# Attention scores by four 64x64 TensorE tiles without the masked quadrants, values four units behind

## The chip, the cores and the metric

The kernel runs on one core of one Trainium2 chip. The metric is the device time of one execution in microseconds (us). Engines are named as in the profile: PE is TensorE's matmul side and PEld its weight loads, DVE is VectorE, ACT ScalarE, POOL GpSimd, SP SyncE.

## What is computed

Three layers on x of shape (4, 2048, 256): a feed-forward layer with ternary weights, attention, and the same feed-forward layer again. The change touches the attention alone:

```python
q = einsum('bld,dhk->blhk', x, Wq) / sqrt(dh)      # 16 heads of 64
k = einsum('bld,dhk->blhk', x, Wk)
v = einsum('bld,dhk->blhk', x, Wv)
# side keys and values: x summed over groups of 16 tokens, 128 groups a batch
# block of 128 queries against 3 * 128 neighbouring keys and 128 side keys
rel = k_idx - bl - q_idx
valid = (abs(rel) <= 127) & (k_pos >= 0) & (k_pos < L)
logits = einsum('bnqhd,bnkhd->bnhqk', qb, k_cat) + bias   # 0, or -1e9 where not valid
probs = softmax_with_extra_logit(logits)
y = einsum('bnhqk,bnkhd->bnqhd', probs, v_cat)
out = einsum('blhk,hkd->bld', y, Wo)
```

A query at place i of its block sees the keys of the left block from place i + 1 on and those of the right block up to place i - 1. So of the left block's keys the first 64 are masked for the last 64 queries, and of the right block's keys the last 64 are masked for the first 64 queries. These are the masked quadrants.

## The kernel before

**Tiling.** The attention works through 64 blocks of 128 tokens, 16 to a batch, in rounds of four blocks (`RING`), so 16 rounds. One head of one block is a unit: 16 units a block, 1024 in all. All loops are written out, so every unit has instructions of its own. Numbers are split in two f16 parts, high and low, and each product is three passes (high x high, high x low, low x high).

**One head.** PE makes the scores of four key tiles of 128 (left, own, right, side, in an order that depends on the block's place in the round, `order_of`) into one of four PSUM banks `score_ps`, 512 columns. DVE adds the mask and takes the largest (L1354). ACT makes the exponentials (L1286). The high part is a copy, by ACT (L1302) for three heads of four and by DVE (L1366) for the fourth. POOL makes the low part (L1013). SP issues one DMA that turns the eight 128x128 f16 tiles of the head (L987); all such issues are on SP's one queue, one behind the other. PE multiplies the turned tiles with the values (`values`, L1147), 12 matmuls of 64 columns. The first block of a batch has no left tile and the last no right one, so three key tiles each.

**How far ahead.** In unit u, SP is to turn head u + 1, POOL to split head u + 2, ACT to make the exponentials of u + 3, DVE to take the largest of u + 4. PE makes the scores of u + 4 to u + 7 in every fourth unit (two pairs of heads), and the values of u - 3 (`PV_LAG`). There are six buffers for the turned tiles, so the issue of head v waits until the values of v - 6 are done.

**The items.** Between these steps PE makes the block's projections in pieces, one or two a unit (`PIECES`): V1, Q0, Q1, K0, K1, V0 for the coming block, OUTP for the one before, and three transposes: XTR turns the normalised x of the block after the next, YT1 and YT0 turn the two halves of y. XTR and YT1 use the bank `y_ps[1]`, which also holds the values of heads 8 to 15. K0 needs XTR's result, the output projection's third piece needs YT1's. Four side items (SK0, SK1, SV0, SV1) come only where a batch begins or ends. `FIRST_ORDER` and `LAST_ORDER` give the items' numbers there. Each item's result is copied out by ACT (high part, L1263) and DVE (low part, L1346).

**Scores in detail.** `scores` takes two heads at once: the even head lies on partitions 0 to 63 of queries and keys, the odd one on 64 to 127, so the two matmuls of a step use the two row halves of the array, 64 rows by 128 columns each. Key tiles that lie side by side in the ring are taken in one matmul. The keys are stored as `k_parts[P, slot, part, HD]`. Every matmul has its own weight load.

**y.** DVE inverts the denominators in units 2 and 10 of a block and scales y in units 3 and 11 (`normalise_y`, L1408).

Of the kernel before, what the change touches and what calls it, by code (L numbers as in the profile page):

```python
# [6 lines left out]
F16 = mybir.dt.float16  # L7
# [8 lines left out]
P = 128  # L16
# [4 lines left out]
H, DH = 16, 64  # L21
# [676 lines left out]
def attention_phase(nc, w):  # L698
# [20 lines left out]

    V1, Q0, XTR, Q1, YT1, K0, OUTP, K1, YT0, V0 = PLAIN = range(10)
    SK0, SK1, SV0, SV1 = range(10, 14)
    FIRST_ORDER = [SK1, V1, Q0, XTR, Q1, SV1, YT1, K0, OUTP, K1, YT0, V0]
    LAST_ORDER = [V1, Q0, XTR, Q1, YT1, K0, SK0, OUTP, K1, YT0, V0, SV0]
    BANK_OF = {V1: 0, Q0: 1, Q1: 0, K0: 0, OUTP: 1, K1: 0, V0: 1, SK1: 1, SV1: 1, SK0: 0, SV0: 0}

    SIDE_LAST, RIGHT_FIRST, OWN_FIRST = ORDERS = ((LEFT, OWN, RIGHT, SIDE_TILE), (RIGHT, LEFT, OWN, SIDE_TILE),
                                                  (OWN, RIGHT, LEFT, SIDE_TILE))
    MASK_OF = {SIDE_LAST: 0, RIGHT_FIRST: 4, OWN_FIRST: 3}  # L730
    PIECES = [[(V1, 0)], [(V1, 1)], [(Q0, 0)], [(Q0, 1)], [(XTR, 0), (Q1, 0)], [(Q1, 1)], [(OUTP, 0)], [(OUTP, 1), (YT1, 0)],
              [(K0, 0)], [(K0, 1)], [(OUTP, 2)], [(OUTP, 3)], [(K1, 0)], [(K1, 1)],
              [(YT0, 0), (V0, 0)], [(V0, 1)]]
    XTR_SLOT = 4
    FIRST_SIDE = {0: SK1, 5: SV1}
    LAST_SIDE = {10: SK0, 15: SV0}
    TURNS = (XTR, YT1, YT0)
# [6 lines left out]
    U = RING * H  # L744
    ROUNDS = BLK_PER_BATCH // RING
    STATS_SLOT, NORM_SLOT = 6, 14
    SCORE_AHEAD, EXP_AHEAD, SPLIT_AHEAD, TURN_AHEAD, PV_LAG = 4, 3, 2, 1, 3
    NBUF = 4
    NPARTS = 6
    CLEARED = 4  # L750
# [8 lines left out]
    with ExitStack() as ctx:  # L759
# [14 lines left out]
        xn = sb("b_x_normed", [P, D], F32)  # L774
        xt = [sb(f"b_xT{n}", [P, KD, 2, P], F16) for n in range(2)]
        qs = sb("q_parts", [P, 2, 2, HD], F16)
        kr = sb("k_parts", [P, RING + 1, 2, HD], F16)
        vr = sb("v_parts", [P, RING + 1, 2, HD], F16)
        probs = [sb(f"probs{n}", [P, 4 * P], F32) for n in range(NBUF)]
        parts_of = [sb(f"probs_split{n}", [P, 2, 4 * P], F16) for n in range(NPARTS)]  # L780
# [39 lines left out]

        var_done, rstd_done, xn_done = sem("b_var_done"), sem("b_rstd_done"), sem("b_xn_done")
        dve_step, cleared, half_set = sem("b_dve_step"), sem("b_cleared"), sem("half_set")
        y_cleared = sem("y_cleared")
        block = ctx.enter_context(nc.Block())

        class At:
# [124 lines left out]
        def tiles_of(at, v):  # L951

            j, place = v // H, place_of(at, v)
            slots = {LEFT: (j - 1) % RING, SIDE_TILE: SIDE, OWN: j % RING, RIGHT: (j + 1) % RING}
            tiles = [(t, slots[key]) for t, key in enumerate(order_of(at, v))]
            return tiles if place == INNER else tiles[1:]

        def flat(at, v):

# [88 lines left out]
        def _(pe):  # L1048
# [53 lines left out]
            def scores(at, v):  # L1102

                j, h = divmod(v, H)
                pair, place = h // 2, place_of(at, v)
                if v >= NBUF:
                    max_done.wait(pe, at.heads + v + 1 - NBUF)
                if h == 0 and v:
                    pe.wait_ge(lo_done, at.item(j - 1, SK0 if place == FIRST else K0) + 1)
                if h == H // 2:  # L1110
                    pe.wait_ge(lo_done, at.item(j, SK1) + 1 if place == FIRST else at.item(j - 1, K1) + 1)
                cols = slice(pair * P, (pair + 1) * P)
                todo, started = tiles_of(at, v), False
                while todo:

                    (t, slot), n = todo[0], 1
                    while n < len(todo) and todo[n][1] == slot + n:
                        n += 1
                    todo = todo[n:]
                    for q_part, k_part in ((HI, HI), (HI, LO), (LO, HI)):  # L1120
                        ends = not todo and q_part == LO
                        even = nc.tensor.matmul(score_ps[v % NBUF][:, t * P:(t + n) * P],  # L1122
                                                qs[0:DH, j % 2, q_part, cols], kr[0:DH, slot:slot + n, k_part, cols],
                                                start=not started, stop=ends, skip_group_check=True)
                        odd = nc.tensor.matmul(score_ps[v % NBUF + 1][:, t * P:(t + n) * P],  # L1125
                                               qs[DH:P, j % 2, q_part, cols], kr[DH:P, slot:slot + n, k_part, cols],
                                               start=not started, stop=ends, skip_group_check=True)
                        started = True
                even.then_inc(scores_done.sem, 1)
                odd.then_inc(scores_done.sem, 1)  # L1130

# [52 lines left out]
            for index, (kind, n) in enumerate(PRE):  # L1184
                if index == FIRST_SCORES:
                    pe.wait_ge(lo_done, FIRST_SCORES)
                    for v in range(0, SCORE_AHEAD, 2):
                        scores(At(0, 0), v)
                if kind == XTR:
                    turn_x(y_ps[0], n)  # L1190
                    continue
                earlier = [m for m in range(index) if PRE_ORDER[m] not in TURNS]
                if len(earlier) > 1:
                    bank_free(index, index - earlier[-2])
                pe.wait_ge(lo_done, PRE.index((XTR, n)) + 1)
                project(kind, pre_bank(index), side_source(0) if kind in (SK0, SV0) else block_source(n))

            def body(at, b):
                for u in range(U):
                    j, h = divmod(u, H)  # L1200
                    if u % NBUF == 0:
                        for pair in range(0, NBUF, 2):
                            scores(at, u + SCORE_AHEAD + pair)
                    side = side_item(at, j, h)
                    if side == SK1:
                        block_item(at, b, j, side, (0, 1))
                    for kind, piece in PIECES[h]:
                        if kind not in TURNS:
                            block_item(at, b, j, kind, (piece,))
                    if h == XTR_SLOT:  # L1210
                        block_item(at, b, j, XTR, (0,))
                    if side in (SK0, SV0, SV1):
                        block_item(at, b, j, side, (0, 1))
                    values(at, u - PV_LAG)
                    for kind, piece in PIECES[h]:
                        if kind in (YT0, YT1):
                            block_item(at, b, j, kind, (piece,))
# [3 lines left out]
            pe.wait_ge(lo_done, PRE_ITEMS)  # L1221
            batches(pe, body)
            end = End()
            values(end, -3)
            values(end, -2)
            values(end, -1)
# [4 lines left out]
        def destination(kind, part, xt_parity, slot):  # L1231

            c = int(kind in SECOND)
            if kind == XTR:
                return xt[xt_parity][:, :, part, :]
            if kind in KEYS:
                return kr[:, slot, part, 512 * c:512 * c + 512]
            if kind in QUERIES:
                return qs[:, slot, part, 512 * c:512 * c + 512]
            if kind in VALUES:  # L1240
                return vr[:, slot, part, 512 * c:512 * c + 512]
            return yt[:, part, 4 * c:4 * c + 4, :]

        def result(kind, bank):
            if kind == XTR:
                return bank[:, 0:KD * P].rearrange("p (k n) -> p k n", k=KD)
            return bank[:].rearrange("p (c n) -> p c n", c=4) if kind in (YT0, YT1) else bank[:]

        def ring_slot(j, kind):

# [79 lines left out]
        def _(dve):  # L1330
# [83 lines left out]
            nc.vector.memset(yt[:, :, 0:NPAIR // 2], 0.0).then_inc(cleared, 1)  # L1414
            statistics(0)
            normalise_x(0, None)
            dve.sem_inc(y_done.sem, 1)
            for index, (kind, n) in enumerate(PRE):
                if index == FIRST_SCORES:
# [17 lines left out]
            def body(at, b):  # L1437
                count["base"], count["n"] = at.round * PER_ROUND + before, 0
                for u in range(U):
                    j, h = divmod(u, H)  # L1440
                    if u % NBUF:
                        split_high(at, u + SPLIT_AHEAD)
                        largest(at, u + SCORE_AHEAD)
                    for n, kind in due(at, u):
                        item(at, n, kind)
                    if u % NBUF == 0:
                        split_high(at, u + SPLIT_AHEAD)
                        largest(at, u + SCORE_AHEAD)
                    if h == STATS_SLOT:
                        moments(at.blocks + j + 3)  # L1450
                    if h == STATS_SLOT + 1:
                        mean_variance()
                        add_eps()
                    if h == NORM_SLOT:
                        normalise_x(at.blocks + j + 3, at.item(j, XTR) + 1)
                    if h in (2, 10):
                        invert_denominators(at, u - 3)
                    if h in (3, 11):
                        normalise_y(at, u - 4, at.before(j) if h == 3 else at.item(j, YT1) + 1)
                    for n, kind in due_late(at, u):  # L1460
                        item(at, n, kind)
                assert count["n"] == PER_ROUND
# [37 lines left out]
```

## Time and profile before

| | us |
|---|---|
| median of 3 runs | 2176.99 |
| lowest, highest | 2176.89, 2182.71 |
| the profiled execution | 2183.18 |
| its span, as the profile has it | 2181.5 |

In the span, the first feed-forward layer runs to about 308 us, the attention from there to about 1922 us, the second feed-forward layer after it. The granted TensorE clock is 0.991 of full speed in the mean. Busy shares over the span: PE 94%, PEld 72%, DVE 86%, ACT 88%, POOL 64%.

How to read it: a busy share says how long an engine had something in it, not that it set the pace. Several engines here are near 90%. A wait in the profile belongs to the engine that stood still, and names what ended it. SP's queue isn't counted as busy at all, and its issues have to be looked at one by one: an issue row gives its start and its length, and a second view the time from issue to landing.

### The profile page before, as it was taken

How to read it: one execution, taken by the hardware profiler on the slowest of the kernel's cores; microseconds unless marked ns; L12 is line 12 of the kernel's file. 1: busy time of each engine (PE TensorE's matmuls, PEld its weight loads, DVE VectorE, ACT ScalarE, POOL GpSimd, SP SyncE). 2: the span in 40 equal slices, each digit the busy share in tenths (PEclk: the TensorE clock that was granted, in tenths of full speed). 3: DMA queues.
4: the chain of work that ended last, by engine and by line, in shares of the span. 5: the costliest groups of instructions: out<-in, count | busy, mean ns of one | idle time of the engine just before them, and what ended most of it. 6: DMA issues, size and time to landing. Idle time of an engine off the chain costs nothing. (4 is left out here: it accounts for less than half of the span.)

```text
span 2181.5 us, 77479 instructions
## 1 busy us (share of the span) xinstructions
PE 2049.6 (94%) x30286; PEld 1567.5 (72%) x30286; DVE 1879.6 (86%) x4646; ACT 1930.1 (88%) x4210; POOL 1406.1 (64%) x1455
## 2 busy tenths in 40 slices
PE   5999979999999999999999999999999999979999
PEld 3666657777777777777777778777777777746666
DVE  7999968889998898898979899998889889867776
ACT  5899958999999899999989999998999999969997
POOL 2444536777787687777767777786777777722221
PEclk9999989999999999999999999999999999989999
DMA  7888837999999899999989999999999999958998
GB/s 210 154 156 153 158 61 124 172 166 176 171 173 171 132 174 170 172 178 168 171 143 162 172 174 169 178 179 152 149 171 172 169 177 175 163 87 177 179 179 182
DMA packets 1341581, 355.54 MB, mean 163 GB/s; under 512 B 1321760, under 2 KB 1340192, under 8 KB 1341216
## 3 DMA queue, kind: packets, MB, share of 16 engines
q1 hardware_dynamic: 1341216, 350.59, 100.4%
q8 instruction: 239, 3.92, 0.7%
q14 instruction: 126, 1.03, 0.2%
HBM read 14.68 MB, written 8.39 MB: 11 GB/s over the span
## 5 line engine op out<-in xcount | busy, mean ns | idle before, releaser
L1013 POOL TENSOR_TENSOR probs_split<-probs,probs_split 128x512 f16<-128x512 f32 (+1 forms) x1026 | 1159.3, 1130 | 385.3 <-ACT probs_split L1302 281.3
L1286 ACT ACTIVATE probs<-probs,minus_max 128x512 f32<-128x512 f32 (+1 forms) x1027 | 717.0, 698 | 27.1 <-DVE minus_max L1354 26.9
L1354 DVE CUSTOM_DVE_ANT_0 probs<-score_ps,mask,neg_qk_scale 128x512 f32<-128x512 f32 (+1 forms) x1028 | 723.5, 716 | 9.6 <-PE score_ps L1125 8.3
L1147 PEld LDWEIGHTS y_ps<-v_parts,probsT 128*128 128x128 f16 x11904 | 457.7, 98 | 149.4 <-DMA probsT<-probs_split 71.1
L1147 PE MATMUL y_ps<-v_parts,probsT 128*128 128x64 f16 x11904 | 514.8, 193 | 51.4 <-DMA probsT<-probs_split 49.8
L1302 ACT ACTIVATE probs_split<-probs 128x512 f16<-128x512 f32 (+1 forms) x770 | 470.2, 611 | 8.5 <-DMA probsT<-probs_split 0.3
L1122 PE MATMUL score_ps<-k_parts,q_parts 64*128 64x384 f16 (+3 forms) x2604 | 371.1, 286 | 4.7 <-DVE k_parts L1346 2.7
L1125 PE MATMUL score_ps<-k_parts,q_parts 64*128 64x384 f16 (+3 forms) x2604 | 371.1, 286 | 0.0
L1122 PEld LDWEIGHTS score_ps<-k_parts,q_parts 64*128 64x128 f16 x2604 | 200.5, 94 | 108.0 <-issue 13.2
L1054 PE MATMUL item_ps<-b_xT,wk_split 128*128 128x128 f16 x3168 | 221.7, 220 | 1.9 <-DVE v_parts L1346 1.5
L1054 PE MATMUL item_ps<-wo_split,yT_parts 128*128 128x256 f16 x1560 | 213.9, 274 | 6.1 <-DVE v_parts L1346 4.6
L1054 PE MATMUL item_ps<-b_xT,wq_split 128*128 128x128 f16 x3120 | 218.2, 220 | 1.2 <-DVE b_xT L1346 0.9
L1054 PE MATMUL item_ps<-wv_split,b_xT 128*128 128x512 f16 x786 | 212.3, 380 | 0.0
L1054 PEld LDWEIGHTS item_ps<-b_xT,wk_split 128*128 128x128 f16 x3168 | 180.3, 98 | 35.7 <-issue 22.1
L1366 DVE CAST probs_split<-probs 128x512 f16<-128x512 f32 (+1 forms) x256 | 181.0, 707 | 27.8 <-ACT probs L1286 27.7
L1125 PEld LDWEIGHTS score_ps<-k_parts,q_parts 64*128 64x128 f16 x2604 | 200.4, 94 | 0.0
L1286 ACT ACTIVATION_READ_ACCUMULATOR probs<-probs,minus_max 128x1 f32 x1027 | 194.2, 189 | 0.0
L1054 PEld LDWEIGHTS item_ps<-b_xT,wq_split 128*128 128x128 f16 x3120 | 178.6, 98 | 18.7 <-issue 12.9
L1054 PEld LDWEIGHTS item_ps<-wo_split,yT_parts 128*128 128x128 f16 x1560 | 135.7, 98 | 19.5 <-DVE v_parts L1346 5.1
L1346 DVE TENSOR_TENSOR yT_parts<-y_ps,yT_parts 128x512 f16<-128x512 f32 x129 | 88.5, 686 | 54.4 <-ACT yT_parts L1263 54.3
L1346 DVE TENSOR_TENSOR v_parts<-item_ps,v_parts 128x512 f16<-128x512 f32 x140 | 95.7, 686 | 43.5 <-ACT v_parts L1263 43.4
L1263 ACT ACTIVATE k_parts<-item_ps 128x512 f16<-128x512 f32 x141 | 84.2, 597 | 53.8 <-PE item_ps L1054 51.5
(172 smaller groups left out, 3452.1 us busy)
## 6 DMA issues: line engine op xcount, KB each, us to landing
probsT<-probs_split SPq DMA_TRANSPOSE x1025, 3.9
out_x<-x_resident SPq DMA_DIRECT2D x64, 128.0 KB, 2.0
x_resident<-in_L_attn_x SPq DMA_DIRECT2D x56, 128.0 KB, 2.7
h_a<-in_L_ffn_w_up SPq DMA_DIRECT2D x1, 1024.0 KB, 5.8
scratch_a<-in_L_ffn_w_down SPq DMA_DIRECT2D x1, 1024.0 KB, 8.0
x_resident<-in_L_attn_x SPq DMA_DIRECT2D x2, 512.0 KB, 9.4
raw_q_a<-in_L_attn_Wq SPq DMA_DIRECT2D x1, 1024.0 KB, 11.5
raw_k_a<-in_L_attn_Wk SPq DMA_DIRECT2D x1, 1024.0 KB, 11.8
```

The source lines that it names most:

```text
L1013: nc.gpsimd.tensor_tensor(parts_of[ring(at, v)][:, LO, low_columns(place_of(at, v))], probs[v % NBUF][:, cols], parts_of[ring(at, v)][:, H ...
L1054: last = nc.tensor.matmul(out, left(k, a), right(k, b), start=(k == 0 and m == 0), stop=(k == n - 1 and m == 2))
L1122: even = nc.tensor.matmul(score_ps[v % NBUF][:, t * P:(t + n) * P], qs[0:DH, j % 2, q_part, cols], kr[0:DH, slot:slot + n, k_part, cols], ...
L1125: odd = nc.tensor.matmul(score_ps[v % NBUF + 1][:, t * P:(t + n) * P], qs[DH:P, j % 2, q_part, cols], kr[DH:P, slot:slot + n, k_part, cols ...
L1147: last = nc.tensor.matmul(out, pt[ring(at, v)][:, low * a + t, :], vr[:, slot, b, h * DH:(h + 1) * DH], start=(n == 0), stop=(n == len(pas ...
L1263: nc.scalar.activation(dst, src, ACT.Copy).then_inc(hi_done, 1)
L1286: nc.scalar.activation(probs[v % NBUF][:, cols], probs[v % NBUF][:, cols], ACT.Exp, bias=bias[:, j % 2, h:h + 1], scale=-1.0, accum_out=su ...
L1302: nc.scalar.activation(parts_of[ring(at, v)][:, HI, cols], probs[v % NBUF][:, cols], ACT.Copy).then_inc(phi_done[v % 4], 1)
L1346: nc.vector.tensor_tensor(dst, src, hi, ALU.subtract).then_inc(lo_done, 1)
L1354: nc.vector.tensor_tensor_reduce(out=probs[v % NBUF][:, cols], in0=score_ps[v % NBUF][:, cols], in1=mask_of(at, v), scale=w.neg_qk_scale[: ...
L1366: nc.vector.tensor_copy(parts_of[ring(at, v)][:, HI, cols], probs[v % NBUF][:, cols]).then_inc(phi_done[v % 4], 1)
```

## The change

Four edits, all in the attention:

1. `scores` cuts each matmul in two halves of the queries, so four tiles of 64 rows by 64 columns are addressed: even and odd head, first and last 64 queries. For the last 64 queries the first 64 keys of the left tile are left out, for the first 64 queries the last 64 keys of the right tile. `key_runs` finds the columns that lie side by side. The keys' layout becomes `[P, part, pair, slot * P]`, so that half a tile and its neighbour are one run; ACT and DVE write them in four pieces of 128.
2. The quadrants left out are never written by PE. So DVE clears the four `score_ps` banks once, before the first item, and PE waits for that before the first scores.
3. `PV_LAG` goes from 3 to 4: PE makes the values of u - 4 in unit u. The inversion and scaling of y move from units 2, 3, 10, 11 to 3, 4, 11, 12.
4. XTR moves from unit 4 to unit 6, ahead of OUTP's first piece, behind Q1 in the items' order; YT1 moves from unit 7 to unit 8.

```diff
-    V1, Q0, XTR, Q1, YT1, K0, OUTP, K1, YT0, V0 = PLAIN = range(10)
+    V1, Q0, Q1, XTR, YT1, K0, OUTP, K1, YT0, V0 = PLAIN = range(10)
-    FIRST_ORDER = [SK1, V1, Q0, XTR, Q1, SV1, YT1, K0, OUTP, K1, YT0, V0]
-    LAST_ORDER = [V1, Q0, XTR, Q1, YT1, K0, SK0, OUTP, K1, YT0, V0, SV0]
+    FIRST_ORDER = [SK1, V1, Q0, Q1, SV1, XTR, YT1, K0, OUTP, K1, YT0, V0]
+    LAST_ORDER = [V1, Q0, Q1, XTR, YT1, K0, SK0, OUTP, K1, YT0, V0, SV0]
-    PIECES = [[(V1, 0)], [(V1, 1)], [(Q0, 0)], [(Q0, 1)], [(XTR, 0), (Q1, 0)], [(Q1, 1)], [(OUTP, 0)], [(OUTP, 1), (YT1, 0)],
-              [(K0, 0)], [(K0, 1)], [(OUTP, 2)], [(OUTP, 3)], [(K1, 0)], [(K1, 1)],
+    PIECES = [[(V1, 0)], [(V1, 1)], [(Q0, 0)], [(Q0, 1)], [(Q1, 0)], [(Q1, 1)], [(XTR, 0), (OUTP, 0)], [(OUTP, 1)],
+              [(K0, 0), (YT1, 0)], [(K0, 1)], [(OUTP, 2)], [(OUTP, 3)], [(K1, 0)], [(K1, 1)],
-    XTR_SLOT = 4
+    XTR_SLOT = 6
-    SCORE_AHEAD, EXP_AHEAD, SPLIT_AHEAD, TURN_AHEAD, PV_LAG = 4, 3, 2, 1, 3
+    SCORE_AHEAD, EXP_AHEAD, SPLIT_AHEAD, TURN_AHEAD, PV_LAG = 4, 3, 2, 1, 4
-        kr = sb("k_parts", [P, RING + 1, 2, HD], F16)
+        kr = sb("k_parts", [P, 2, NPAIR, (RING + 1) * P], F16)
+        def key_runs(at, v, side):
+
+            order, runs = order_of(at, v), []
+            for t, slot in tiles_of(at, v):
+                first = DH if order[t] == LEFT and side == 1 else 0
+                end = DH if order[t] == RIGHT and side == 0 else P
+                to, source, n = t * P + first, slot * P + first, end - first
+                if runs and runs[-1][0] + runs[-1][2] == to and runs[-1][1] + runs[-1][2] == source:
+                    runs[-1][2] += n
+                else:
+                    runs.append([to, source, n])
+            return runs
@@ scores
-                cols = slice(pair * P, (pair + 1) * P)
-                todo, started = tiles_of(at, v), False
-                while todo:
...
-                    for q_part, k_part in ((HI, HI), (HI, LO), (LO, HI)):
-                        ends = not todo and q_part == LO
-                        even = nc.tensor.matmul(score_ps[v % NBUF][:, t * P:(t + n) * P],
-                                                qs[0:DH, j % 2, q_part, cols], kr[0:DH, slot:slot + n, k_part, cols],
-                                                start=not started, stop=ends, skip_group_check=True)
-                        odd = nc.tensor.matmul(score_ps[v % NBUF + 1][:, t * P:(t + n) * P],
-                                               qs[DH:P, j % 2, q_part, cols], kr[DH:P, slot:slot + n, k_part, cols],
-                                               start=not started, stop=ends, skip_group_check=True)
+                runs = [key_runs(at, v, side) for side in range(2)]
+                last = {}
+                for q_part, k_part in ((HI, HI), (HI, LO), (LO, HI)):
+                    for run in range(max(map(len, runs))):
+                        for side in range(2):
+                            if run >= len(runs[side]):
+                                continue
+                            queries = slice(pair * P + side * DH, pair * P + (side + 1) * DH)
+                            to, source, n = runs[side][run]
+                            ends = q_part == LO and run == len(runs[side]) - 1
+                            for odd in range(2):
+                                rows = slice(odd * DH, (odd + 1) * DH)
+                                last[odd] = nc.tensor.matmul(
+                                    score_ps[v % NBUF + odd][side * DH:(side + 1) * DH, to:to + n],
+                                    qs[rows, j % 2, q_part, queries], kr[rows, k_part, pair, source:source + n],
+                                    start=(run == 0 and q_part == k_part), stop=ends, skip_group_check=True)
@@ PE, before the first scores, and DVE, before the first item
+                    pe.wait_ge(scores_cleared, NBUF)
+            for n in range(NBUF):
+                nc.vector.memset(score_ps[n][:], 0.0).then_inc(scores_cleared, 1)
@@ DVE, each unit
-                    if h in (2, 10):
-                        invert_denominators(at, u - 3)
                     if h in (3, 11):
-                        normalise_y(at, u - 4, at.before(j) if h == 3 else at.item(j, YT1) + 1)
+                        invert_denominators(at, u - 4)
+                    if h in (4, 12):
+                        normalise_y(at, u - 5, at.before(j) if h == 4 else at.item(j, YT1) + 1)
```

## Rows read from the trace of the kernel before

**Rows 1.** Busy us (instructions): PE, PEld, DVE, ACT, POOL; clock, DMA share, GB/s

```profile
400.00:1800.00 1400.00, 1347.96 (x23400) 1068.58 (x23398) 1242.18 (x3066) 1286.54 (x3124) 1075.80 (x1075) 1.00 1.11 168
```

**Rows 2.** Waits, 400 to 1800 us: who for whom, total us, times, longest

```profile
PEld y_ps L1147 <- DMA probsT<-probs_split: 62.4, 110, 1.6
...
PE y_ps L1147 <- DMA probsT<-probs_split: 44.4, 80, 1.4
...
PEld score_ps L1122 <- DVE minus_max L1354: 5.8, 23, 0.5
```

**Rows 3.** Timeline of SP's queue: start us, us; whole attention, then single issues

```profile
327.33 1592.27 SPq L987 DMA_TRANSPOSE probsT<-probs_split  x1025
...
955.14 1.28 SPq L987 DMA_TRANSPOSE probsT<-probs_split  x1
...
956.51 1.29 SPq L987 DMA_TRANSPOSE probsT<-probs_split  x1
...
959.44 2.19 SPq L987 DMA_TRANSPOSE probsT<-probs_split  x1
...
961.72 1.28 SPq L987 DMA_TRANSPOSE probsT<-probs_split  x1
```

**Rows 4.** Tile probsT, two windows of 100 us, then landing over the attention

```profile
L987 SPq DMA_TRANSPOSE probsT<-probs_split x66: 1232/1288/2722, 799.1 to 899.6; - x66
...
L987 SPq DMA_TRANSPOSE probsT<-probs_split x65: 1232/1290/2582, 899.6 to 998.0; - x65
...
DMA to landing us min/median/max: 2.7/3.9/6.0
```

**Rows 5.** DMA traffic in the stretches of the issues at 955.14 and 959.44

```profile
DMA packets 933, 0.23 MB, mean 193 GB/s; under 512 B 933, under 2 KB 933, under 8 KB 933
...
DMA packets 620, 0.17 MB, mean 83 GB/s; under 512 B 619, under 2 KB 619, under 8 KB 619
...
q8 instruction: 1, 0.02, 2.8%
```

**Rows 6.** Queue q8: packets, MB; 400:1800, 327:1920, 800:900 and 900:1000 us

```profile
q8 instruction: 184, 3.01, 0.9%
...
q8 instruction: 209, 3.42, 0.9%
...
q8 instruction: 14, 0.23, 0.9%
...
q8 instruction: 13, 0.21, 0.8%
```

**Rows 7.** Timeline of PE: values, transposes of y, loads and matmuls of scores

```profile
900.36 0.51 PE L1147 MATMUL y_ps<-v_parts,probsT 128*128 128x64 f16 x12
...
902.99 0.64 PE L1087 MATMUL y_ps<-ident,y 128*128 128x128 f32 x4
...
904.55 0.09 PEld L1122 LDWEIGHTS score_ps<-k_parts,q_parts 64*128 64x128 f16 x1
904.55 0.09 PEld L1125 LDWEIGHTS score_ps<-k_parts,q_parts 64*128 64x128 f16 x1
...
904.67 0.22 PE L1122 MATMUL score_ps<-k_parts,q_parts 64*128 64x128 f16 x1
...
904.73 0.32 PE L1122 MATMUL score_ps<-k_parts,q_parts 64*128 64x384 f16 x1
...
904.89 0.32 PE L1122 MATMUL score_ps<-k_parts,q_parts 64*128 64x384 f16 x1
```

**Rows 8.** Groups by line and form, 300 to 1900 us: busy us, mean ns

```profile
L1147 PE MATMUL y_ps<-v_parts,probsT 128*128 128x64 f16 x11771 | 509.1, 193 | 49.9 <-DMA probsT<-probs_split 48.3
...
L1087 PE MATMUL y_ps<-ident,y 128*128 128x128 f32 x504 | 80.0, 281 | 0.0
...
L1263 ACT ACTIVATE b_xT<-y_ps 128x256 f16<-128x256 f32 x65 | 24.2, 372 | 17.0 <-PE y_ps L1080 16.8
...
L1413 DVE MEMSET y_ps<- 128x512 f32 x1 | 0.5, 485 | 0.5 <-PEq L84 0.5
```

More of the change, by code:

```diff
@@ L822, in attention_phase @@
         dve_step, cleared, half_set = sem("b_dve_step"), sem("b_cleared"), sem("half_set")
-        y_cleared = sem("y_cleared")
+        y_cleared, scores_cleared = sem("y_cleared"), sem("scores_cleared")
         block = ctx.enter_context(nc.Block())
@@ L1111, in scores @@
                     pe.wait_ge(lo_done, at.item(j, SK1) + 1 if place == FIRST else at.item(j - 1, K1) + 1)
-                cols = slice(pair * P, (pair + 1) * P)
-                todo, started = tiles_of(at, v), False
-                while todo:
[L1116 to L1119, printed above, removed]
-                    for q_part, k_part in ((HI, HI), (HI, LO), (LO, HI)):
-                        ends = not todo and q_part == LO
-                        even = nc.tensor.matmul(score_ps[v % NBUF][:, t * P:(t + n) * P],
-                                                qs[0:DH, j % 2, q_part, cols], kr[0:DH, slot:slot + n, k_part, cols],
-                                                start=not started, stop=ends, skip_group_check=True)
-                        odd = nc.tensor.matmul(score_ps[v % NBUF + 1][:, t * P:(t + n) * P],
-                                               qs[DH:P, j % 2, q_part, cols], kr[DH:P, slot:slot + n, k_part, cols],
-                                               start=not started, stop=ends, skip_group_check=True)
-                        started = True
@@ L1129, in scores @@
+                even, odd = last[0], last[1]
                 even.then_inc(scores_done.sem, 1)
@@ L1206, in body @@
                         block_item(at, b, j, side, (0, 1))
+                    if h == XTR_SLOT:
+                        block_item(at, b, j, XTR, (0,))
                     for kind, piece in PIECES[h]:
@@ L1209, in body @@
                             block_item(at, b, j, kind, (piece,))
-                    if h == XTR_SLOT:
-                        block_item(at, b, j, XTR, (0,))
                     if side in (SK0, SV0, SV1):
@@ L1223, in _ @@
             end = End()
+            values(end, -4)
             values(end, -3)
@@ L1236, in destination @@
             if kind in KEYS:
-                return kr[:, slot, part, 512 * c:512 * c + 512]
+                return kr[:, part, 4 * c:4 * c + 4, slot * P:(slot + 1) * P]
             if kind in QUERIES:
@@ L1246, in result @@
                 return bank[:, 0:KD * P].rearrange("p (k n) -> p k n", k=KD)
-            return bank[:].rearrange("p (c n) -> p c n", c=4) if kind in (YT0, YT1) else bank[:]
+            return bank[:].rearrange("p (c n) -> p c n", c=4) if kind in (YT0, YT1, *KEYS) else bank[:]
         def ring_slot(j, kind):
```

## The prediction

> **What bounds the kernel now.** I read the page's shares first, then the attention alone, its waits, and then the DMA issues one by one. The shares point at TensorE: in the 1400 us between 400 and 1800 it is busy 1347.96 us (96.3%), ScalarE 91.9%, VectorE 88.7%, at a granted clock of 1.00, the 2.4 GHz level [rows 1]. PE has 52 us of idle time there. The waits say what ends it: nearly always the landing of a transposed probability tile (44.4 us on the matmul side, 62.4 us on the weight side, the same stalls seen twice); for VectorE's maxima PE waits 5.8 us [rows 2].
>
> A late transpose can be latency or throughput. Latency: 3.9 us from issue to landing [rows 4], and PE uses a tile four units of work after SyncE's turn for it. Throughput: the 1025 issues fill 1592.27 us, 1.553 us each [rows 3], and one head is one issue. Single issues show how full that queue is. The reader is to see that the one at 955.14 takes 1.28 us and that the next starts 0.09 us after its end (956.42 to 956.51): 1.38 us a head with nothing in the way. The one at 959.44 takes 2.19 us, 0.9 more, and its successor again starts 0.09 us behind it (961.63 to 961.72) [rows 3]. In the stretch of the long one the DMA engines move 83 GB/s instead of 193, and one packet of queue q8, an instruction packet, is on them [rows 5].
>
> Whose instructions are these? Between 400 and 1800 q8 brings 3.01 MB in 184 packets [rows 6], 16.4 kB each, while PE runs 23400 matmuls and 23398 weight loads [rows 1]: 46798/184 = 254 a packet. No other engine has such numbers: q8 fetches PE's program, some 256 instructions at a time.
>
> What does a fetch cost SyncE? From 799.1 to 899.6 us lie 65 steps between issues and 14 fetches: (100.5 - 65 x 1.38)/14 = 0.77 us. From 899.6 to 998.0 lie 64 steps and 13 fetches: 0.78 us [rows 4, 6]. These hold whatever idle time the queue had. I take 0.75; as bounds 0.9, the single issue above, and 0.5, if one fetch in three falls between issues. Over the attention: 1025 x 1.38 = 1415 us and 209 fetches [rows 6] x 0.75 = 157 us, 1572 of 1592 us. In only about 20 us had SyncE's queue nothing to issue. **The transposing queue is the bound**, and PE the close second: its idle time is what the queue leaves it.
>
> **The change part by part.** *Scores.* Before, a pair of heads is 12 matmuls (6 where the key tiles lie in one run), even and odd head on the two row halves at once: the next starts 0.16 us after 384 columns and 0.06 after 128 [rows 7], so 3 x (0.16 + 0.06) = 0.66 us a pair. After, each is cut into two halves of the queries, and each half drops 64 of 512 key columns. By the runs that the code finds, a pair becomes 24 matmuls in the first, second and fourth block of a round (before 12), 18 in the third (6), 12 in the last block of a batch (6); over the phase 5208 become 11184. If the four tiles overlap, a pair lasts as long as one half: 320 columns are 0.135 us at the same rate, 3 x (0.135 + 0.06) = 0.585 us, 0.075 less, 512 x 0.075 = 38 us less PE work. PE is not the bound: 0 in the sum.
>
> *Instructions.* 5976 more matmuls and, since loads equal matmuls [rows 1], 5976 more loads are 11952 instructions, 11952/256 = 46.7 more fetches, each 0.75 us of SyncE's queue: **+35 us**; bounds +23 and +42.
>
> The Trainium skill, "Runtime: NRT & Kernel Launch", section "Instruction fetch mechanics", says that a program is refilled in blocks of 256 instructions over a DMA queue of the engine's own, and that crossing a block is "mostly hidden". The trace agrees on the 256; for the transposes on the same DMA engines it does not show the hiding. By the page the term would be 0 instead of 35.
>
> *Can the tiles overlap?* Two row halves do: weight loads and matmuls of both start within 0.01 us [rows 7]. Column halves and loads of 64 columns stand in no row. Fast end: the values' loads of 128 columns recur every (0.51 - 0.193)/11 = 0.029 us. Slow end: fp32 loads recur every (0.64 - 0.281)/3 = 0.12 us with their transposes [rows 7, 8], so 0.06 us for half the columns. With column halves loading in turn, four loads take at most 0.12 us, less than a run of 320 columns and more than one of 128: at worst 3 x (0.135 + 0.12) = 0.77 us a pair. PE has 52/1400 x 1.553 = 0.058 us to spare a head and gets 35/1024 = 0.034 more from the slower queue, 0.18 a pair: it binds only from 0.66 + 0.18 = 0.84 us a pair. I take 0, the nearer rows being the fast ones; the other side is a rival.
>
> *Values four units behind.* A tile gets 1.55 us more to land, but the queue serves no more tiles per us. It can win back the 20 us in which the queue was empty, in the fill and where a batch changes and PE has the side items too: **-12 us** (bounds 0 and -20). New wait: the issue of head v needs the values of v - 6 done. Tile v - 6 lands 6 x 1.55 - 3.9 = 5.4 us before that issue, which leaves them time; were that gone, each us would be one of the bound, for all behind it in SyncE's queue.
>
> *x turned at unit 6, YT1 at unit 8, normalisation one unit later.* K0 at unit 8 needs the turned x: four units of cover become two, 3.1 us, against two transposes and two copies, ACT's 0.37 us [rows 8] and DVE's of the same 256 columns. YT1 has two units until the output projection's third piece instead of three. Both hidden; if not, under 1 us a block, out of PE's spare time. Keys are stored in four pieces of 128, the same elements: 0.
>
> *Clearing four score banks.* Four memsets of 0.485 us [rows 8] on VectorE in the fill, partly beside PE's first transposes: **+1 us** (0 to 2).
>
> Sum: 35 - 12 + 1 = **+24 us**; bounds 23 - 20 = +3 and 42 + 2 = +44. The profiled execution took 2183.18 us, 2181.5 of it span, 6.2 us above the median of the runs. So 2207 in a profile, and 2176.99 + 24 = 2201 us as median.
>
> **The rivals.** *Faster: PE bounds.* If SyncE's long issues were waits that shrink when tiles come evenly, the extra unit removes PE's idle time (1593/1400 x 52 = 59 us) and the scores save up to 38, of which ScalarE's 91.9% lets most through, say 30: 2177 - 59 - 30 = 2088 us. For: 96.3%. Against: 0.09 us between issues, and the packet in the long one. It decides where SyncE's gaps are well over 0.09 us. 0.12.
>
> *No change.* Fetches fall between issues (0.5 us each) and all 20 us come back: +3, 2180 us. 0.18.
>
> The page's rule on fetches would give 2177 - 12 = 2165 us, for which I leave 0.05 of the 0.12 above.
>
> *Much slower: the four tiles take turns.* Column halves one after the other make 2 x 0.585 = 1.17 us a pair, 0.51 more, 261 us of PE work against its 59 + 35 us of room: +35 + 167, about 2379 us. Against: row halves overlap. It decides from 0.84 us a pair. 0.10.
>
> The Trainium skill gives a load as its columns/1.2 in ns ("TensorE: Matmul & The Clock Gate", section "LDWEIGHTS (loading the stationary operand)"), 53 ns for 64, and says that column tiling turns the fast load off ("TensorEngine Tiling (Array Packing)", "Restrictions"); 24 in turn would be 1.27 us a pair, on this rival's side.
>
> *The change doesn't do what it says.* If repeated weights were not loaded again, the fetches would grow by 23 only, about +6 us; but the loads equal the matmuls today [rows 1]. It is within the 0.18.
>
> **How the numbers follow.** Forecast 0.60, no change 0.18, faster 0.12, much slower 0.10. The range takes the sum's bounds (2180 to 2221), goes down over no change and the page's case to 2165, and up to 2245 for loads that cost PE part of its room. About 0.3%, 6.5 us, is what a measurement tells from no change: faster 0.12, same 0.18, slower 0.70.
>
> **What would show it.** Right: some 47 more q8 packets, issues 1.58 us apart in the mean with ordinary ones still at 1.29, a lower busy share of PE with longer waits for landed tiles, scores in fours 0.135 us apart. Wrong: gaps in SyncE's queue, a mean step under 1.55 us, or score pairs over 0.84 us with PE over 98% busy.

## The result and the profile after

The changed kernel takes 2211.45 us (median of 4 runs, 2209.7 to 2217.48) against 2179.85 us of the kernel before beside it: a ratio of 1.0152, 95% interval 1.0132 to 1.0172. It is slower by 1.5%, 32 us. The forecast was 2201 us and a loss of 24. The profiled execution has a span of 2208.0 us where the one before had 2181.5.

The two instruction queues on the page of the changed kernel (packets, MB, share of 16 engines), and then the packets of q8 in its attention, 400 to 1800 us:

```profile
q8 instruction: 286, 4.69, 0.9%
q14 instruction: 126, 1.03, 0.2%
...
q8 instruction: 221, 3.62, 1.1%
```

q8 has 47 packets more than the 239 it had, as 11952 more instructions of PE make it, and q14, the other instruction queue, has as many as before. Next, the changed kernel's windows view (busy us of PE, PEld, DVE, ACT, POOL, then clock, DMA share and GB/s), the line that answers to [rows 1]:

```profile
400.00:1800.00 1400.00, 1316.59 (x28184) 1107.09 (x28182) 1208.42 (x3014) 1264.29 (x3070) 1052.98 (x1056) 1.00 1.13 165
```

PE is busy for 94.0% instead of 96.3% while it runs 28184 matmuls instead of 23400; every other computing engine is less busy too, at the same clock. No engine became the bound: the whole attention got less to do per us. The timeline of SyncE's queue in the changed kernel answers to [rows 3], and the DMA traffic in the stretches of its first three single issues to [rows 5]:

```profile
327.08 1620.72 SPq L1000 DMA_TRANSPOSE probsT<-probs_split  x1025
...
959.14 1.29 SPq L1000 DMA_TRANSPOSE probsT<-probs_split  x1
...
960.53 2.15 SPq L1000 DMA_TRANSPOSE probsT<-probs_split  x1
...
962.77 1.28 SPq L1000 DMA_TRANSPOSE probsT<-probs_split  x1
```

```profile
q8 instruction: 1, 0.02, 6.8%
...
DMA packets 673, 0.17 MB, mean 86 GB/s; under 512 B 673, under 2 KB 673, under 8 KB 673
...
DMA packets 962, 0.24 MB, mean 219 GB/s; under 512 B 962, under 2 KB 962, under 8 KB 962
```

The same picture as before: an ordinary issue 1.28 or 1.29 us, the next 0.09 us behind it, and one of 2.15 us at 86 GB/s (its instruction packet began in the stretch ahead of it). The 1025 issues took 1620.72 us instead of 1592.27, **28.5 us more**, which is the loss of the profiled execution (26.5 us) and a little more. The mean step is not stretched evenly; only more issues are long: of the 1025, the trace has 223 over 1.6 us where the kernel before had 190, and 219 of them (189 before) have an instruction packet of q8 that starts in them or less than 1.4 us ahead. Nor is the pair of stretches above a chance find. Lined up on the starts of all 221 packets of q8 between 400 and 1800 us, the transposes start about 190 packets of their own in each quarter of a microsecond beforehand, and about 10 in the quarters from 1.0 to 1.5 us afterwards; over the 184 of the kernel before it is the same. In the tile view of probsT, 400 to 1800 us, the median issue is 1288 ns, as it was, and there are 890 issues where there were 906:

```profile
L1000 SPq DMA_TRANSPOSE probsT<-probs_split x890: 1209/1288/2643, 399.0 to 1799.5; - x178
```

One view seems to speak against a full queue. For the kernel before it has SyncE waiting for GpSimd's low parts half of the time:

```profile
SPq L987 <- POOL probs_split L1013: 769.5, 819, 21.1
```

That is only the last releaser that the profile could name. Matched head by head, each low part was done before its issue began, by 1.37 us in the median before and by 2.36 us after the change. So the tiles stood ready and the queue was late.

The scores themselves came out as hoped. One burst of four heads in the changed kernel, and the last matmuls of such a burst in the kernel before, which began at 904.55 [rows 7]:

```profile
920.89 1.35 PE L1137 MATMUL score_ps<-k_parts,q_parts 64*64 64x64 f16 x48
```

```profile
905.71 0.32 PE L1122 MATMUL score_ps<-k_parts,q_parts 64*128 64x384 f16 x1
```

Before, 24 matmuls took from 904.55 to 906.03, 1.48 us; now 48 take 1.35. Less the 0.19 us that the last one needs to drain, 1.29 and 1.16 us: 0.58 us a pair of heads, where 0.585 was forecast. Four tiles of 64x64 do overlap.

Waits of the changed kernel, 400 to 1800 us (who for whom, total us, times, longest):

```profile
PEld item_ps L1067 <- DVE yT_parts L1361: 59.6, 98, 1.6
PE item_ps L1067 <- DVE yT_parts L1361: 45.8, 56, 1.5
...
PEld y_ps L1160 <- DMA probsT<-probs_split: 37.0, 66, 1.3
ACT probs_split L1317 <- DMA probsT<-probs_split: 31.8, 60, 1.4
...
DVE probs_split L1381 <- DMA probsT<-probs_split: 21.2, 22, 2.0
...
PE y_ps L1160 <- DMA probsT<-probs_split: 19.2, 41, 1.0
```

PE's waits for landed tiles became shorter, not longer (44.4 and 62.4 us before, [rows 2]). With one unit more between transpose and use, the stall is met further up: ACT and DVE now wait for a landing before they may overwrite the buffer that is being turned. PE's wait for the turned y has another source in the main: it is 26.8 to 30.0 us also in the kernels below in which the transposes no longer bound.

### The profile page after: what moved, and what is told of

The parts are those of the page before. It is cut to its first block and busy times, and to the rows that moved or that the text cites. A ratio compares the mean times of both kernels' runs of the same rounds, so it can differ in the third digit from the quotient of the medians.

```text
span 2208.0 us, 89437 instructions
## 1 busy us (share of the span) xinstructions
PE 2036.7 (92%) x36262; PEld 1631.0 (74%) x36262; DVE 1868.9 (85%) x4650; ACT 1929.3 (87%) x4210; POOL 1402.8 (64%) x1455
## 5 line engine op out<-in xcount | busy, mean ns | idle before, releaser
L1317 ACT ACTIVATE probs_split<-probs 128x512 f16<-128x512 f32 (+1 forms) x770 | 470.8, 611 | 46.7 <-DMA probsT<-probs_split 37.3
L1137 PE MATMUL score_ps<-k_parts,q_parts 64*64 64x128 f16 (+6 forms) x11184 | 353.5, 266 | 11.0 <-DVE minus_max L1369 3.1
L1137 PEld LDWEIGHTS score_ps<-k_parts,q_parts 64*64 64x64 f16 x11184 | 253.7, 106 | 61.0 <-DVE minus_max L1369 24.5
L1381 DVE CAST probs_split<-probs 128x512 f16<-128x512 f32 (+1 forms) x256 | 161.4, 630 | 54.8 <-ACT probs L1301 31.6
L1361 DVE TENSOR_TENSOR q_parts<-item_ps,q_parts 128x512 f16<-128x512 f32 x130 | 89.5, 688 | 76.0 <-ACT q_parts L1278 76.0
L355 DVE TENSOR_TENSOR h_split_c<-h_c,h_split_c 128x1024 f16<-128x1024 f32 x64 | 78.4, 1225 | 58.2 <-ACT h_split_c L660 57.0
L282 POOL TENSOR_TENSOR h_rms_c<-mean_square_c,pow_exp_c 128x4 f32<-128x4 f32 x16 | 16.5, 1030 | 165.2 <-ACT scratch_c L664 165.2
```

Of the source, the lines that this page charges most:

```text
L1137: last[odd] = nc.tensor.matmul(score_ps[v % NBUF + odd][side * DH:(side + 1) * DH, to:to + n], qs[rows, j % 2, q_part, queries], kr[rows, ...
L1317: nc.scalar.activation(parts_of[ring(at, v)][:, HI, cols], probs[v % NBUF][:, cols], ACT.Copy).then_inc(phi_done[v % 4], 1)
L1361: nc.vector.tensor_tensor(dst, src, hi, ALU.subtract).then_inc(lo_done, 1)
L1381: nc.vector.tensor_copy(parts_of[ring(at, v)][:, HI, cols], probs[v % NBUF][:, cols]).then_inc(phi_done[v % 4], 1)
```

## The experiments

All ratios are to runs of the kernel before on the same chip. **Fetch theory**: the transposes bound the attention, and each fetch of 256 PE instructions takes some 0.7 us from them. Its rivals: PE bounds; or the moved items are slow.

### The scores alone

The four-tile scores and the cleared banks, with the rest as before (the main lines of the edit against the changed kernel):

```diff
-    SCORE_AHEAD, EXP_AHEAD, SPLIT_AHEAD, TURN_AHEAD, PV_LAG = 4, 3, 2, 1, 4
+    SCORE_AHEAD, EXP_AHEAD, SPLIT_AHEAD, TURN_AHEAD, PV_LAG = 4, 3, 2, 1, 3
-    XTR_SLOT = 6
+    XTR_SLOT = 4
```

> The change's four-tile scores and the cleared banks alone; values three units behind, x and y turned where the kernel before has them. Fetch theory (SyncE's transposing queue bounds, and each fetch of PE's instructions stretches one of its issues): 46.7 more fetches, each 0.5 to 0.9 us, so +23 to +42 us against the kernel before, q8 286 packets, no idle time in SyncE's queue inside a batch. Rival 1, PE bounds: about -38 us, since PE's work falls. Rival 2, it is the later values and turns that cost the time: within 6 us of the kernel before.

Measured: ratio 1.0148 (1.012 to 1.0175), 2211.36 us, q8 286 packets. The whole loss is here, +32 us by the ratio, and it comes with less work on PE's array. PE's waits for landed tiles grew, as forecast for the whole change (scores-only kernel, 400 to 1800 us; its profiled execution, 2199.69 us, was the fastest of its four):

```profile
PEld y_ps L1160 <- DMA probsT<-probs_split: 106.4, 164, 1.8
...
PE y_ps L1160 <- DMA probsT<-probs_split: 72.3, 126, 1.6
```

### The lag and the moved items alone

```diff
-    SCORE_AHEAD, EXP_AHEAD, SPLIT_AHEAD, TURN_AHEAD, PV_LAG = 4, 3, 2, 1, 3
+    SCORE_AHEAD, EXP_AHEAD, SPLIT_AHEAD, TURN_AHEAD, PV_LAG = 4, 3, 2, 1, 4
-    XTR_SLOT = 4
+    XTR_SLOT = 6
```

> The other half of the change alone: values four units behind, x turned at unit 6, y at unit 8, y scaled a unit later; scores as before. Fetch theory: q8 stays at 239 packets and the queue stays full, so only its idle time of some 20 us can come back, of which the changed kernel shows little: -12 to +3 us. Rival 1, PE bounds: -40 to -59 us, its waits for landed tiles being its loss. Rival 2, the later turn of y costs the time: +6 to +35 us.

Measured: ratio 1.0011 (0.9997 to 1.0025). PE's waits for landed tiles are all but gone, and a wait for the turned y stands in their place (lag-only kernel, 400 to 1800 us):

```profile
PE item_ps L1054 <- DVE yT_parts L1347: 29.2, 57, 1.1
...
PE y_ps L1147 <- DMA probsT<-probs_split: 1.3, 3, 0.7
```

Taken alone this run doesn't tell whether PE bounds: a gain by the later values could be hidden by a loss from the moved items, and the same kernel with the transposes relieved (below) takes 2177.32 us, only 6 us less. The cleaner comparison is the changed kernel with the scores-only kernel. They differ by the same half of the change, the ratios are 1.0152 and 1.0148, and here the changed kernel with the transposes relieved lies 40 us lower, at 2170.83. There too nothing is won by letting tiles land later, and nothing of the queue's idle time comes back.

### More instructions without the scores

The values' projection in eight matmuls of 64 columns instead of one of 512:

```diff
-                    last = parts(bank[:], source, lambda k, s: w.wqkv[2][:, s, k, cols], pieces, KD)
+                    for k in pieces:
+                        for m, (a, o) in enumerate(((HI, HI), (HI, LO), (LO, HI))):
+                            for r in range(8):
+                                last = nc.tensor.matmul(bank[:, 64 * r:64 * r + 64], source(k, a),
+                                                        w.wqkv[2][:, o, k, 512 * c + 64 * r:512 * c + 64 * r + 64],
+                                                        start=(k == 0 and m == 0 and r == 0),
+                                                        stop=(k == KD - 1 and m == 2), skip_group_check=True)
```

> The kernel before, with each matmul of the values' projection (128 x 512) cut in eight of 64 columns: the same sums, 5502 more matmuls and as many weight loads, scores untouched. PE's work grows by 48 x 0.029 - 6 x 0.216 = 0.11 us for each of 131 items, 14 us. Fetch theory: 11004/256 = 43 more fetches, +22 to +39 us, middle 30, q8 282 packets. Rival 1, PE bounds: +14 us. Rival 2, instruction fetches are hidden and PE has room: within 6 us of the kernel before.

Measured: ratio 1.0135 (1.0114 to 1.0156), +29 us, with 285 packets on q8. Two edits that share nothing but some 11000 to 12000 added PE instructions, half of them weight loads, cost the same. Per added packet: 32.3/47 = 0.69 us in the scores-only kernel, 29.4/46 = 0.64 us here. PE's own 14 us would not do. That the added loads slow the transposes by themselves, without a fetch, doesn't fit the single issues: the ordinary one keeps its length (1288 ns in the median), and 222 are over 1.6 us, all 222 of them with an instruction packet of q8.

### The transposes relieved: every fourth head not turned

```diff
             def turn_probs(at, v):
 
+                if (at.heads + v) % 4 == 3:
+                    return
...
-                pe.wait_ge(turned[ring(at, v)], turn_count(at, v))
+                src = v - int(v % 4 == 3)
+                pe.wait_ge(turned[ring(at, src)], turn_count(at, src))
```

> The kernel before without the transpose of every fourth head; that head's values are made from its predecessor's turned tiles (so its output is not the reference's), all other work stays. Fetch theory: SyncE's queue needs 769 x 1.38 + 209 x 0.75 = 1218 us and no longer bounds; PE's idle time (59 us) goes: -40 to -59 us against the kernel before, PE over 98% busy. Rival, the transposes don't bound the pace: within 10 us of it.

> The same with the changed kernel: no transpose of every fourth head, whose values come from its predecessor's tiles. Fetch theory: with the queue relieved PE bounds, and its shorter scores count: 10 to 38 us faster than the relieved kernel before, so -60 to -95 us against the kernel before. Rival, the four tiles or the moved items are slow by themselves: slower than the relieved kernel before by 10 to 30 us.

Measured: the relieved kernel before 0.9684 (0.9661 to 0.9707), 2113.14 us. 71 us are gained with PE's, DVE's and ACT's work unchanged, more than the 59 at most that I had for PE's idle time. PE's busy time had stalls in it too: it was 1347.96/23400 = 57.6 ns a matmul before and is 1393.82/24541 = 56.8 ns here. Its windows row (columns as above) shows PE at 99.6% and DMA's share at 0.87 instead of 1.11:

```profile
400.00:1800.00 1400.00, 1393.82 (x24541) 1122.35 (x24540) 1288.82 (x3212) 1337.78 (x3271) 1127.33 (x1126) 1.00 0.87 133
```

But the relieved changed kernel reached only 0.9946 (0.9926 to 0.9966), 2170.83 us: 58 us slower than the relieved kernel before, where I expected it 10 to 38 us faster and my rival 10 to 30 us slower. So the change holds a second loss, hidden as long as the transposes bound. The halves of the change, relieved in the same way, tell which part it is:

> The scores-only kernel (four-tile scores, values three units behind, turns as before) without the transpose of every fourth head, whose values come from its predecessor's tiles. Theory A: with the queue relieved the four-tile scores are a gain (two pairs took 1.153 us in the changed kernel, 1.293 before), and the changed kernel's loss in the relieved state comes from the moved items: 10 to 36 us faster than the relieved kernel before (2113 us). Theory B, the scores cost the time even then: 2150 to 2175 us.

> The lag-only kernel (scores as before, values four units behind, x and y turned later) without the transpose of every fourth head. Theory A, the moved items cost the time once the queue is relieved: 2160 to 2195 us, with PE waiting at the output projection for the turned y. Theory B: 2105 to 2120 us, as the relieved kernel before.

Measured: scores only 0.9626 (0.96 to 0.9651), 2103.56 us; lag only 0.9968 (0.9956 to 0.9979), 2177.32 us. Beside the relieved kernel before (2113) the scores gain 10 us and the moved items lose 64. In the relieved lag-only kernel PE waits for the turned y where in the relieved kernel before it hardly did, and ACT waits for PE to turn it (400 to 1800 us):

```profile
ACT yT_parts L1268 <- PE y_ps L1090: 58.6, 59, 2.1
...
PEld item_ps L1057 <- DVE yT_parts L1351: 43.3, 83, 0.6
...
PE item_ps L1057 <- DVE yT_parts L1351: 26.8, 57, 0.5
```

PE's own wait of 26.8 us is less than half of the 64, so this line alone doesn't account for them.

Unit 8 opens with the scores of four heads. YT1 in unit 8 so comes a unit and a burst later, and two units before the output projection that needs it. The last run put YT1 back to unit 7. It also moved XTR from unit 6 to unit 5, so two items differ from the relieved changed kernel (the lines of `PIECES` cut short):

```diff
-    PIECES = [... [(Q1, 0)], [(Q1, 1)], [(XTR, 0), (OUTP, 0)], [(OUTP, 1)],
-              [(K0, 0), (YT1, 0)], [(K0, 1)], ...
+    PIECES = [... [(Q1, 0)], [(Q1, 1), (XTR, 0)], [(OUTP, 0)], [(OUTP, 1), (YT1, 0)],
+              [(K0, 0)], [(K0, 1)], ...
-    XTR_SLOT = 6
+    XTR_SLOT = 5
```

> The changed kernel with x turned at unit 5 behind Q1 and YT1 back at unit 7 (values still four units behind), and, as in the other relieved kernels, without the transpose of every fourth head, whose values come from its predecessor's tiles. In unit 8 PE makes the scores of four heads first (1.15 us), so YT1 there comes a unit and a score burst later, two units ahead of the output projection that needs it. Theory A, YT1's place is what costs the moved items their 57 to 64 us: 2095 to 2120 us, PE's waits for yT_parts near 0. Theory B, it is the values' lag of four or the later scaling of y: 2150 to 2175 us as the relieved changed kernel (2171).

Measured: 0.9781 (0.9756 to 0.9806), 2133.41 us, between the two forecasts. The waits for yT_parts are small now, and another has come (400 to 1800 us):

```profile
PEld y_ps L1096 <- DVE y L1427: 41.2, 58, 0.8
PE y_ps L1096 <- DVE y L1427: 30.8, 55, 0.6
...
PEld item_ps L1070 <- DVE yT_parts L1365: 10.0, 56, 0.3
```

37 of the 58 us came back. As the wait that shrank is the one for the turned y, YT1's place is the likely cause, but XTR moved too, and no run moves YT1 alone. 30 us still lie between this kernel and the relieved scores-only one. PE's wait of 30.8 us at XTR for the scaled y would account for them, but x turned at unit 5 with y scaled a unit later is this run's own doing, so how the rest divides in the change itself (whose XTR is at unit 6) stays open.

### Is it the issuing or what lies behind it?

One wait less in SyncE's queue, with GpSimd waiting in its place:

```diff
-                pv_done.wait(sp, at.heads + v - NPARTS)
@@ split_low
+                pv_done.wait(pool, at.heads + v - NPARTS)
```

> The kernel before, with the wait for the values of v - 6 moved from SyncE's queue to GpSimd's, ahead of the low part that SyncE waits for anyway. All work and all orders stay. Before, each issue starts 0.092 us after the end of the last, with one waiting instruction of its own between; without it I expect 0.046. Fetch theory, the queue bounds: 1024 x 0.046 = 47 us less of it, of which PE's 59 us of room allow nearly all: -30 to -47 us. Rival, the queue only looks full: within 6 us of the kernel before.

> The scores-only kernel with the same moved wait. Fetch theory: the fetches' 30 us stay, the wait's 47 go, and PE has room for all of it: -12 to -22 us against the kernel before, so slower by 15 to 35 us than the kernel before with the moved wait. Rival, PE bounds as soon as the queue is shorter: faster than that one by up to 36 us.

Measured: 0.9984 (0.9968 to 0.9999) and 1.012 (1.0092 to 1.0148). My two forecasts against the kernel before (-30 to -47 us and -12 to -22 us) fell; I had named the wrong part of the queue. The difference between the two kernels held: 33 us, where 15 to 35 were forecast for the fetches. The time of the first is also what its rival said, a queue that only looks full; single issues tell the two apart. Three issues of the first kernel, and its tile view, 400 to 1800 us:

```profile
950.83 1.34 SPq L986 DMA_TRANSPOSE probsT<-probs_split  x1
...
952.21 1.33 SPq L986 DMA_TRANSPOSE probsT<-probs_split  x1
...
953.58 1.33 SPq L986 DMA_TRANSPOSE probsT<-probs_split  x1
```

```profile
L986 SPq DMA_TRANSPOSE probsT<-probs_split x910: 1209/1336/2742, 398.4 to 1799.8; - x182
```

The gap between issues fell from 0.09 to 0.04 us, as expected, and the issue itself grew from 1288 to 1336 ns. The step stays at 1.38 us. A queue with time to spare would have shown the 48 ns as idle time; here the issue took them up. So SyncE is held by what takes its transposes, and an issue's length is partly a wait for that. The pace of 1.38 us for a head of eight tiles is then one of the DMA side, and the fetches of instructions cut into that pace, not into SyncE's time. Which part of the DMA side sets it, no run tells.

Two heads in one issue of 16 tiles, on the changed kernel and on the lag-only one:

```diff
-                for u in range(U):
-                    turn_probs(at, u + TURN_AHEAD)
+                for u in range(0, U, 2):
+                    turn_probs(at, u)
...
+                sp.dma_start_transpose(pair_turned[n][:], pair_parts[n][:].rearrange("p h s n -> p (h s n)")).then_inc(turned[n], 16)
```

> The changed kernel with the tiles of two heads turned by one DMA issue of 16 tiles (two issues of one head each in the first and last block of a batch); six buffers as before. Same result, same bytes. If an issue costs SyncE a fixed time (an issue of 6 tiles took 1.21 to 1.24 us and one of 8 tiles 1.29), 16 tiles take about 1.5 us, the queue is half empty and PE bounds: -60 to -95 us against the kernel before. Rival, the DMA engines are the bound, not the issuing: an issue takes 2.6 us and the time stays within 15 us of the changed kernel's.

> The same two-heads issue with the scores of the kernel before (values four units behind, as in the lag-only kernel). With a fixed time for an issue: -30 to -59 us against the kernel before, and slower than the two-heads kernel with four-tile scores by 10 to 38 us. Rival, the DMA engines are the bound: within 15 us of the kernel before, and faster than the two-heads kernel with four-tile scores by some 30 us.

Measured: 1.0207 (1.0184 to 1.023), 2227.95 us, and 1.0173 (1.0153 to 1.0193), 2220.95 us. No gain came, so both forecasts for a fixed time of an issue fell. Of the rival's, one held: by the ratios the first kernel is some 12 us from the changed one (within 15). The second is 38 us slower than the kernel before, not within 15, and 7 us faster than the first, not 30. The second kernel's issues of two heads (first line) and of one head, 400 to 1800 us:

```profile
L1001 SPq DMA_TRANSPOSE probsT<-probs_split x394: 1315/2017/3542, 401.7 to 1798.4; - x197
...
L997 SPq DMA_TRANSPOSE probsT<-probs_split x96: 1209/1237/2792, 710.4 to 1575.1; - x96
```

16 tiles can be issued in 1.3 us, the median is 2.0, less than 2 x 1.38 and than the rival's 2.6. The queue has gaps here, of 0.60 us in the median over the attention where they were 0.09 before, so the loss comes from elsewhere. What it is was not tested: both kernels contain the moved items with their hidden loss, and with six buffers ACT waits 46.1 us for landings in this stretch. Whether larger issues help with the old item order and more buffers stays open.

## Why the prediction was right, and where not

**What bounds.** Right in substance. That PE at 96% was only second is shown from three sides: less PE work made the kernel slower (scores only), fewer transposes made it faster by 71 us, and later use of the tiles did nothing (changed kernel against scores only). The step that failed is the naming of the place: "1.38 us a head with nothing in the way" was read as SyncE's own 1.29 us of issuing and 0.09 us between. The kernel with one wait less showed that only the sum of 1.38 is fixed. The forecast did not depend on it, since it used the sum.

**Fetches.** Right, and the term that made the result. 46.7 more were forecast, 47 came (46 of them in the attention); the price was set at 0.75 us and came out at 0.69 and 0.64 us. Measured for the term, +32 us against +35. The Trainium skill ("Runtime: NRT & Kernel Launch", "Instruction fetch mechanics") has blocks of 256 instructions, with which the trace agrees (254 to a packet), and a cost that is "mostly hidden", with which it agrees for PE alone (99.6% busy in the relieved kernel before, with 193 fetches in those 1400 us); for the transposes each costs 0.64 to 0.69 us.

**The idle time of the queue.** Wrong: -12 us forecast, +2 us measured in the lag-only kernel (interval -1 to +5), and within 1 us between the scores-only and the changed kernel by the ratios, of which each is good to some 5 us. The idle time itself was there. Added up over the attention, the gaps between issues beyond the usual 0.09 us were 29 us before, 33 in the lag-only kernel, 25 in the scores-only and 27 in the changed one; later values did not close them, and why is not shown. This term is why 24 was forecast and 32 came.

**Scores.** Right: 0.58 us a pair, no cost from loads of 64 columns, 0 in the sum. Their worth where PE does bound was overrated. Of 0.07 x 512 = 36 us only 10 showed in the relieved kernels. In the relieved scores-only kernel PE is still busy for 99.2% and ACT for 96.1% of the stretch, and why the rest did not show, no run tests:

```profile
400.00:1800.00 1400.00, 1388.92 (x30286) 1176.57 (x30284) 1289.48 (x3231) 1345.78 (x3295) 1135.81 (x1133) 1.00 0.92 134
```

**Moved items.** "Both hidden; if not, under 1 us a block, out of PE's spare time" was right for this change, where they cost nothing, but by luck: the transposes covered them, not the units that I counted. The price without that cover was about right too: 64 us over 64 blocks is 1.0 us a block, with the values' lag and the later scaling in it. Units of 1.55 us each are a poor measure, as they aren't alike: every fourth opens with a score burst.

**What would show it.** The mean step was forecast at 1.58 us and is (1799.5 - 399.0)/889 = 1.575. PE's waits for landed tiles became shorter, not longer; that sign was right for the scores-only kernel alone. In the changed kernel the stall stands at ACT and DVE, and at the output projection the moved items have a wait of their own.

**Rivals.** That PE bounds is refuted by the scores-only kernel, the cut projection and the relieved kernel before. That the tiles take turns is refuted by the bursts: 0.58 us a pair and not 1.17. That fetches are hidden is refuted by the scores-only kernel and the cut projection.

## What to carry to other kernels

Look at the single issues of a queue that engines wait for: here a constant small gap between them told of a full queue, whatever the busy shares and the view of SyncE's waits said. In this kernel, which is written out and turns tiles by DMA all the time, each packet of 254 instructions on PE cost the DMA side about 0.65 us, so an edit that makes PE's work shorter by more and smaller instructions lost. And measure each half of an edit with the present bound relieved as well: a loss of 64 us was hidden behind the transposes and would have met whoever removed them next. A half that shows no effect, as the lag-only kernel did, can be a gain and a loss that cancel, or a second limit close to the first.

## What the runs showed of the hardware

With each instruction packet of 16 kB the transposes in flight came nearly to a stop, a microsecond after its start: all 16 DMA engines together moved 86 GB/s instead of 219 in two stretches of the same 4 us, and in the mean over 221 packets the transposes' traffic was at about a twentieth (10 packets a quarter us instead of 190) from 1.0 to 1.5 us after the packet's start. An issue's length in the trace is not its cost: 1288 ns became 1336 when 48 ns ahead of it were removed. The four tiles of 64x64 overlapped fully: 24 matmuls (each tile one of 64 and one of 384 columns, or one of 128 and one of 320, three times) with as many weight loads in 0.58 us, 24 ns for each pair of instructions, less than the 29 ns between full-width matmuls of 64 columns with their loads.
